# Products that nothing reads in two stretches of TensorE, and expert weights moved behind the exponent queries, in a two-layer gated cross-attention kernel

## The reference

```python
x = x + tanh(g_xattn[0]) * attention0(layernorm(x), ctx)            # softmax over 1500 keys
x = x + tanh(g_ffn[0])   * experts0(layernorm(x))                   # 8 experts, 128 -> 512 -> 128, gelu, top 2
x = x + tanh(g_xattn[1]) * attention1(layernorm(x), ctx, mask)
x = x + tanh(g_ffn[1])   * (experts1(layernorm(x)) + shared(layernorm(x)))   # 8 experts, 128 -> 64 -> 128
```

## Time and profile before

| | us |
|---|---|
| median of 3 runs | 1026.82 (1025.94 to 1027.41) |
| the profiled execution | 1026.83 |
| its span, first to last instruction | 1025.0 |
| PE busy | 905.8 (88%) |
| DVE busy | 731.6 (71%) |
| ACT busy | 588.3 (57%) |
| POOL busy | 518.1 (51%) |

### The profile page before, as it was taken

How to read it: one execution, slowest core, us unless ns; L and a number is a source line. 1 busy time by engine, 2 the same in 40 slices (tenths; PEclk the granted TensorE clock), 3 DMA queues, 4 the chain that set the end, 5 groups by cost and what they waited for, 6 DMA issues and landing times.

```text
span 1025.0 us, 32567 instructions
## 1 busy us (share of the span) xinstructions
PE 905.8 (88%) x13088; PEld 654.5 (64%) x13088; DVE 731.6 (71%) x1579; ACT 588.3 (57%) x1076; POOL 518.1 (51%) x662
## 2 busy tenths in 40 slices
PE   3887788898989899898999999999999999999975
PEld 1364576676766667677666777666666666666754
DVE  5665666777868678686775867788787878787723
ACT  1154547565575755757556575665657675757560
POOL 5542436643545445354744556666657666672211
PEclk9997899999999999999999999999999999999995
DMA  5324451222212222212665666677566666675300
GB/s 140 89 81 136 140 152 37 84 69 80 70 51 72 73 80 80 67 53 67 138 121 101 124 119 147 131 144 155 127 153 131 137 130 148 140 139 94 59 2 19
DMA packets 100291, 104.47 MB, mean 102 GB/s; under 512 B 28251, under 2 KB 93101, under 8 KB 100141
## 3 DMA queue, kind: packets, MB, share of 16 engines
q1 hardware_dynamic: 98722, 102.07, 42.6%
q10 hardware_dynamic: 1418, 0.32, 0.2%
HBM read 35.89 MB, written 0.46 MB: 35 GB/s over the span
## 4 chain that ended last, share of the span: by engine, by line
PE 57%; DVE 25%; ACT 9%; issue 7%; DMA 1%; SPq 0%; ACTq 0%; DVEq 0%
DVE mx L1056 13%; PE pO L1191 13%; PE pMX L1212 10%; PE pST L1170 8%; PE pKV L1257 6%; PE pKV L1248 6%; PE pFH L1379 5%; PE pFY L1311 3%; ACT P L773 3%; DVE rden L998 2%; ACT HR L782 2%; ACT L773 2%; DVE HR L954 2%; PE pFY L1315 2%; DVE ysc L1027 1%
## 5 line engine op out<-in xcount | busy, mean ns | idle before, releaser
L1056 DVE TENSOR_REDUCE mx<-pMX 112x1 f32<-112x500 f32 x768 | 487.5, 669 | 133.9 <-PE pMX L1212 131.1
L773 ACT ACTIVATE P<-pST 125x448 f32<-125x448 f32 x768 | 389.4, 542 | 286.7 <-PE pST L1170 281.5
L1212 PE MATMUL pMX<-kop,qmax 48*112 48x500 f16 (+1 forms) x768 | 285.9, 412 | 47.9 <-DVE mx L1056 38.1
L1170 PE MATMUL pST<-qexp,kop 50*128 50x112 f16 (+2 forms) x3072 | 267.7, 216 | 20.3 <-issue 10.1
L1170 PEld LDWEIGHTS pST<-qexp,kop 50*128 50x128 f16 (+2 forms) x3072 | 184.3, 101 | 86.0 <-issue 30.8
L1191 PE MATMUL pO<-P,V 125*17 125x112 f32 x6144 | 189.0, 264 | 0.0
L1212 PEld LDWEIGHTS pMX<-kop,qmax 48*112 48x112 f16 (+1 forms) x768 | 97.9, 130 | 123.1 <-DVE mx L1056 59.0
L630 POOL CAST khi<-kfull 128x500 f16<-128x500 f32 x96 | 57.9, 603 | 206.5 <-ACT kfull L800 205.1
L1191 PEld LDWEIGHTS pO<-P,V 125*17 125x17 f32 x6144 | 138.4, 98 | 35.0 <-issue 19.3
L632 POOL TENSOR_TENSOR klo<-kfull,khi 128x500 f16<-128x500 f32 x96 | 109.0, 1136 | 7.8
L721 POOL TENSOR_TENSOR Clo<-C,Chi 128x500 f16<-128x500 f32 x93 | 106.0, 1139 | 7.5
(11 more groups left out here) (152 smaller groups left out, 1112.8 us busy)
## 6 DMA issues: line engine op xcount, KB each, us to landing
C<-in_ctxT SPq DMA_DIRECT2D x31, 750.0 KB, 5.8
kop<-maskop SPq DMA_DIRECT2D x48, 437.5 KB
kop<-khi SPq DMA_DIRECT2D x192, 62.5 KB
kop<-khi SPq DMA_DIRECT2D x96, 125.0 KB
kop<-klo SPq DMA_DIRECT2D x96, 62.5 KB
kop<-klo SPq DMA_DIRECT2D x48, 125.0 KB
maskin<-in_mask SPq DMA_DIRECT2D x8, 656.2 KB, 5.9
qexp<-qmax SPq DMA_DIRECT2D x16, 182.0 KB
```

The source lines that it names most:

```text
L773: nc.scalar.activation(P[0:KP, slot, h * 4 * T:(h + 1) * 4 * T], pST[0:KP, h, 0:4 * T], ACT.Exp, scale=EXP_SCALE).then_inc(exp_done, 1)
L1056: nc.vector.tensor_reduce(mx[:, s % 2, c, p:p + 1], pMX[0:T, m % 2, 0:CW], AX.X, ALU.max).then_inc(max_done, 1)
L1170: mm = nc.tensor.matmul(pST[0:keys.stop - keys.start, h, i * T:(i + 1) * T], kop[rows, b, slot, keys], qexp[rows, b, slot, :, :].rearrange ...
L1212: nc.tensor.matmul(pMX[0:T, m % 2, 0:CW], qmax[rows, b, slot, :, :].rearrange("r j q -> r (j q)"), kop[rows, b, slot, c * CW:(c + 1) * CW] ...
```

## The change

Five groups of edits.

- **Fillers.** `keep_busy(bank, n)` issues n products of a 128 x 128 identity with 512 columns (fp16) into a PSUM bank that nothing reads at that time; no wait and no signal. In step 0 eight go ahead of round 0, two ahead of rounds 1, 3, 5, 7 and 11; in steps 33 and 34 `in_gap` names how many follow which small product.
- **Expert weights.** Loads of one expert each (256 KB) go right behind `qexp<-qmax`: `w1a` in steps 1 and 2, `w2a` in 3 and 4; `w1b` in step 5, `w2b` in 6. PE waits for them by pairs of experts. Biases and the first mask stay in `late_loads(1)`.
- **Start.** The first transfer brings `wk0` and `wq0`. The query weights and biases are no longer scaled; `head_of` holds 4.0 instead of 1.0, so that q is scaled as it is masked. The reordering of `wq0` is done by ACT after its first context piece. Key piece 0 of batch 0 is issued ahead of the context of batch 1.
- **Constants.** `late_constants` is split: `masks()` runs behind `other_weights()` in step -1, `output_biases()` (8 + 2 operations) in round 8 of step 1. Their loads move on ACT from round 11 of step 0 to round 8 of step -1.
- **Waits.** The counts follow from the above.

```diff
+def in_gap(s, use):
+    return {(NB + 1, "sum"): 5, (NB + 1, "y3"): 10, (NB + 1, "xT"): 2, (NB + 1, "h1"): 10,
+            (NB + 2, "gT"): 2, (NB + 2, "y1"): 3}.get((s, use), 0)
...
-            sp.dma_start(W[:, 0:D], wpack[:, 0:D]).then_inc(wk_in, 16)
+            sp.dma_start(W[:, 0:2 * D], wpack[:, 0:2 * D]).then_inc(wk_in, 16)
...
                 if s == 1:
...
-                    sp.dma_start(w1a[:, 0:E0 // 2, :], w1_0[0:E0 // 2].rearrange("e d f -> d e f")).then_inc(f_in, 16)
                     sp.dma_start(maskin[:, :], mask[0]).then_inc(mask_in, 16)
-                if s == 2:
-                    sp.dma_start(w1a[:, E0 // 2:, :], w1_0[E0 // 2:].rearrange("e d f -> d e f")).then_inc(f2_in, 16)
+            def expert_weights(s):
+                if s in (1, 2):
+                    for e in range(4 * (s - 1), 4 * s):
+                        sp.dma_start(w1a[:, e, :], w1_0[e]).then_inc(w1_in[e // 2], 16)
+                if s in (3, 4):
+                    for e in range(4 * (s - 3), 4 * (s - 2)):
+                        sp.dma_start(w2a[:, e, :, :], w2_0[e].rearrange("(c f) d -> f c d", c=F0C)
+                                     ).then_inc(w2_in[e // 2], 16)
+                if s == 5:
                     sp.dma_start(w1b[:, :, :], w1_1.rearrange("e d f -> d e f")).then_inc(f2_in, 16)
+                if s == 6:
                     sp.dma_start(w2b[:, :, :], w2_1.rearrange("(c e) f d -> (e f) c d", e=2)).then_inc(f2_in, 16)
-                if s == 3:
-                    for half in (slice(0, E0 // 2), slice(E0 // 2, E0)):
-                        sp.dma_start(w2a[:, half, :, :], w2_0[half].rearrange("e (c f) d -> f e c d", c=F0C)
-                                     ).then_inc(f3_in, 16)
...
                                      ).then_inc(qexp_in[s % 2], 16)
+                expert_weights(s)
+                if s == -1:
+                    key_chunk(st, 1, 0)
...
+                if c == 0:
+                    act.wait_ge(init_k, 2)
+                    nc.scalar.activation(w("wk0").rearrange("d (h r p) -> d h r p", r=PR, h=2),
+                                         w("wq0").rearrange("d (r h p) -> d h r p", r=PR, h=2), ACT.Copy).then_inc(init_q, 1)
...
-                if s == 0 and kt == 11:
+                if s == -1 and kt == 8:
...
-                nc.vector.memset(head_of[quarter, 0, k % 2:k % 2 + 1], 1.0).then_inc(init_h, 1)
+                nc.vector.memset(head_of[quarter, 0, k % 2:k % 2 + 1], QK_SCALE).then_inc(init_h, 1)
...
-                scaled("wq0", 2 * D).then_inc(init_v, 1)
-                dve.wait_ge(init_v, 3)
-                dve.wait_ge(init_k, 2)
-                nc.vector.tensor_copy(w("wk0").rearrange("d (h r p) -> d h r p", r=PR, h=2),
-                                      w("wq0").rearrange("d (r h p) -> d h r p", r=PR, h=2)).then_inc(init_b, 1)
...
-                    if s == 2 and kt == 2:
-                        late_constants()
+                    if s == 1 and kt == 8:
+                        output_biases()
...
+            def keep_busy(bank, n):
+                for _ in range(n):
+                    nc.tensor.matmul(bank[:, 0, :], ident16[:, :], Whi[:, :, :, :].rearrange("p l m n -> p (l m n)"),
+                                     start=True, stop=True)
...
+                    if s == 0:
+                        keep_busy(pST, 8 if kt == 0 else 0 if kt in (2, 4, 6, 8, 9, 10) else 2)
...
                         small(use)
+                        keep_busy(pMX, in_gap(s, use))
...
                             mm.then_inc(fh_ready, 1)
+                            keep_busy(pMX, in_gap(s, use))
```

More of the change, by code:

```diff
@@ L391, in build @@
         x0_in, c0_in = sem("x0_in"), [sem(f"c0_in{c}") for c in range(CH)]
-        w_in, x_in, f_in, f2_in, f3_in, wo_in = sem("w_in"), sem("x_in"), sem("f_in"), sem("f2_in"), sem("f3_in"), sem("wo_in")
+        w_in, x_in, f_in, f2_in, wo_in = sem("w_in"), sem("x_in"), sem("f_in"), sem("f2_in"), sem("wo_in")
+        w1_in, w2_in = [sem(f"w1_in{i}") for i in range(4)], [sem(f"w2_in{i}") for i in range(4)]
         c_in = sem("c_in")
@@ L395, in build @@
         init_chi = sem("init_chi")
-        init_k, init_b, init_clo = sem("init_k"), sem("init_b"), sem("init_clo")
+        init_k, init_q, init_b, init_clo = sem("init_k"), sem("init_q"), sem("init_b"), sem("init_clo")
         chi_done = sem("chi_done")
@@ L473, in _ @@
                 sp.dma_start(C[:, c * CW:(c + 1) * CW], ctxT[0, :, c * CW:(c + 1) * CW]).then_inc(c0_in[c], 16)
-            sp.dma_start(W[:, D:], wpack[:, D:]).then_inc(w_in, 16)
+            sp.dma_start(W[:, 2 * D:], wpack[:, 2 * D:]).then_inc(w_in, 16)
             sp.dma_start(X[:, D:].rearrange("t (g d) -> t g d", g=G - 1),
@@ L481, in late_loads @@
                 if s == 1:
+                    sp.wait_ge(init_w, 4)
                     sp.dma_start(b2x[0:NE, 0, :], b2_0).then_inc(f_in, 16)
@@ L564, in step @@
                 if has_k(s):
-                    key_chunk(st, 1, 0)
+                    if s >= 0:
+                        key_chunk(st, 1, 0)
                     if has_q(s) and s >= 0:
@@ L761, in early_loads @@
                         act.dma_start(bvE[rows, :, :], bvc.rearrange("l g i r -> g i l r")[g]).then_inc(wo_in, 16)
+                if s == 0 and kt == 11:
                     act.wait_ge(bc_in, 16)
@@ L851, in _ @@
                 quarter = slice(32 * k, 32 * (k + 1))
-                nc.vector.memset(head_of[quarter, 0, k % 2:k % 2 + 1], 1.0).then_inc(init_h, 1)
+                nc.vector.memset(head_of[quarter, 0, k % 2:k % 2 + 1], QK_SCALE).then_inc(init_h, 1)
             for j in range(2):
-                nc.vector.memset(head_of[64 * j:64 * (j + 1), 1, j:j + 1], 1.0).then_inc(init_h, 1)
+                nc.vector.memset(head_of[64 * j:64 * (j + 1), 1, j:j + 1], QK_SCALE).then_inc(init_h, 1)
             def scaled(name, width):
@@ L899, in other_weights, with masks @@
                 split_weights(0, 1, init_c, 0)
-                dve.wait_ge(init_v, 5)
+                dve.wait_ge(init_v, 4)
                 for m in range(2):
                     split_weights(1, m, init_c, 2 + 2 * m)
-            def late_constants():
+            def masks():
+                dve.wait_ge(init_p, 12)
                 nc.vector.memset(ones[:, :], 1.0).then_inc(init_l, 1)
@@ L911, in late_constants, with output_biases @@
                 dve.wait_ge(init_l, 5)
+                for j in range(2):
+                    nc.vector.tensor_scalar(headmask[:, :, j, :], ones[:, :].rearrange("p (r q) -> p r q", r=2),
+                                            rowmask[:, j:j + 1], rowmask[:, 2:3], ALU.mult, ALU.add).then_inc(init_l, 1)
+            def output_biases():
                 dve.wait_ge(wo_in, 16 * 8)
                 dve.wait_ge(init_a, 1)
+                dve.wait_ge(init_l, 7)
                 for j in range(2):
@@ L1122, in step @@
                         low_context(0)
-                        query_weights()
+                        key_bias()
                         low_context(1)
@@ L1128, in step @@
                         other_weights()
+                        masks()
                     if has_q(s) and s + 1 >= B and kt == 2:
@@ L1217, in step @@
                 if s == 0:
-                    pe.wait_ge(init_v, 5)
+                    pe.wait_ge(init_v, 4)
                     pe.wait_ge(init_c, 6)
@@ L1221, in step @@
                     pe.wait_ge(init_l, 17)
-                    pe.wait_ge(f_in, 16 * 5)
-                if s == 4:
-                    pe.wait_ge(f2_in, 16 * 3)
+                    pe.wait_ge(f_in, 16 * 4)
+                if s == 8:
+                    pe.wait_ge(f2_in, 16 * 2)
                 def free(sem_, uses, name):
@@ L1296, in small @@
                     else:
-                        if use == "y0" and s == 4:
-                            pe.wait_ge(f3_in, 32)
+                        if s == 4 or s == 5:
+                            pe.wait_ge(w2_in[int(use[1])], 32)
                         if use == "y0" or use == "y1" and layer_of(s - 3) == 0:
@@ L1334, in step @@
                         small("y1")
+                        keep_busy(pMX, in_gap(s, "y1"))
                         score_half(st, kt, 0)
@@ L1369, in step @@
                             if s == -1:
-                                pe.wait_ge(init_b, 3)
+                                pe.wait_ge(init_q, 1)
+                                pe.wait_ge(bias_in, 16 * 5)
                             nc.tensor.matmul(pFH[:, 0:T], wq, xnqT[:, :], start=True, stop=False)
@@ L1376, in step @@
                             l = layer_of(s - 2 if s % 2 else s - 3)
+                            if s == 3 or s == 4:
+                                pe.wait_ge(w1_in[e // 2], 32)
                             if l == 0:
```

9 lines of the change are left out of this document (3 added, 6 removed).

## The result

The changed kernel takes 1014.32 us, median of 4 runs (1012.67 to 1015.93), against 1026.38 us (1024.52 to 1027.41) for the kernel before: a ratio of 0.9884, 95% interval 0.9861 to 0.9908. It is faster, as forecast, but by 12 us instead of 33, and 1014.32 lies above the range, which ended at 1008. The profiled execution took 1013.41 us with a span of 1011.6 us, 13.4 us less than the span before.

A forecast was written before the change was run, and what follows sets the result against it. Early steps and the end were taken as bound by PE's waits, mainly for small ct transfers behind bulk loads, and the low clock behind them. Gains 2.7 + 3.5 + 5.0 + 7.5 + 5.4 + 4.4 + 4.5 = 33.0 gave 993.8 us, range 986 to 1008.

The forecast's parts named there:

- the place of the expert weights: Steps 3 and 4: no bulk load ahead of ct, so waits and low clock shrink; gains 5.4 and 4.4 us.
- The third rival: Weights in four small transfers hold up context and keys, about 2 us in each of four steps; 1001.8 us, chance 0.08.
- The start: Up to the first maximum product: less DVE work and waiting brings q earlier; gain 2.7 us, bounds 1.5 and 3.5.
- I take -3.5 us, a rise early in step 0: Step 0: fillers raise the clock early, making projections and maximum products faster; 3.5 us gained.
- the first rival: Step 0's fillers don't raise the clock; step 0 loses 3.4 us, step 1 0.8; 1006.5 us, chance 0.25.
- my best case: Step 0: full clock from the outset, -6.0 + 1.7 = -4.3 us.
- if the clock is up on entry: Step 1: full clock gives 6 us, less 1 us for moved output biases; gain 5.0 us.
- the term of the clock: Step 2: a shorter stall no longer takes the clock down, so low-clock work shrinks; 4 us of the 7.5 gained.
- wrong if a fall follows the mask in step 2: Step 2: sign against the forecast, which expected about 25 us and no low clock there.
- The fourth rival: Steps 2 to 4: ct late for another reason, stalls and low clock stay; 15.5 us less gain, 1009.3 us, chance 0.06.
- fillers at full clock, at 0.22 us each: The end: fillers hold the clock, saving 5.2 us for 0.7 us of cost; gain 4.5 us.
- The second rival: The end falls to the lower clock despite fillers: 7.0 us lost instead of 4.5 gained; 1005.3 us, chance 0.08.

The follow-up runs named there:

- the spread kernels: Changed kernel with context load first, step 0's fillers spread behind maximum products, with or without fillers in step 1: 1002.57 us with, 1005.61 us without.
- the kernel with all that helped: Changed kernel with context load first, spread fillers in steps 0 and 1, and denser fillers at the end: 996.75 us, ratio 0.9704 to the kernel before.
- the last two kernels: The kernel with all that helped, 996.75 us, and the same with the first mask's load moved to step 4, 998.98 us.

## Why the prediction was right in part, and wrong in its sum

**Right: the place of the expert weights.** Steps 3 and 4 gained 5.4 and 4.2 us where 5.4 and 4.4 were forecast. The working was that the bulk load ahead of `ct` makes the wait and the wait takes the clock down; the kernel with the old place shows both again. How much of it was the wait and how much the low clock behind it isn't shown: in steps 3 and 4 both went together. The cost of the 16 issues was put at nothing and was nothing: in steps 3 and 4 PE's waits for DMA are too short to be listed, and its longest wait of any kind is 0.7 us. The third rival (small transfers slow) is refuted by the kernel with single large ones, 1015.94 against 1014.32 us. Its premise, four landings one behind the other (12.4 us), was wrong: a group is in after some 5.7 us.

On that rival the Trainium skill, "DMA: Bandwidth & Descriptors", section "Bandwidth", had its rule of at least 1 MiB a transfer. No run here shows a loss from it: a 256 KB transfer takes 3.7 us, a 1024 KB one 5.8 us, and the kernel's time is the same.

**The start: the term was mis-sized, since one edit was left out of it.** The prediction took q, its issue and its landing to move together, and it gave no price to key piece 0 going ahead of the context load. In the timeline of SP in the kernel before, that load is issued well ahead of the queries, which go out from 15.55 us:

```profile
12.38 0.33 SPq L563 DMA_DIRECT2D C<-in_ctxT  x1
12.82 1.34 SPq L514 DMA_DIRECT2D kop<-khi  x2
```

The change moved it to 15.38 us, into the midst of the queries. The earlier issue is real (16.29 instead of 19.85 us at its end); the landing gave 2.7 of the 3.5 us back. With the context first the first maximum product is at 18.57 us, 3.5 us earlier than before, and at 18.13 us without fillers ahead of it: more than the forecast. What was missed is the very thing the prediction used for `ct`: a small urgent transfer behind bulk.

**Step 0: the step that failed is "I take -3.5 us, a rise early in step 0".** The rise came, earlier than I had hoped: the first maximum product took 0.42 us. What I didn't ask is what follows the rise. The eight fillers end at 19.0 us, then PE stands 2.29 us for the late queries, then come maximum products with waits for DVE between them; the clock is low again from 23 us on. With the context first the eight have no wait behind them, only the sparse maximum products, and the clock falls all the same, 3.4 us after its rise at 18.1 us. From there the first rival's price applied: a pair takes 1.0 us (26.33 to 27.32) instead of 0.43, with DVE waiting. It was bounded at +3.4 us; measured are +2.1 us (27.23 against 25.15 us without fillers). The size of the term was right for a clock that holds: 20.5 us in the spread kernels is -4.8 us, where my best case was -4.3.

**Step 1** failed with it, by the same sentence ("if the clock is up on entry"). It was up at 48.5 us, but fell at 50.3. The stretch ahead of that holds only maximum products and the waits for DVE's maxima: PE is busy for 3.46 of the 5.63 us from 44.57 to 50.20 us. With one or two fillers behind each product there PE is busy 5.39 of 5.66 us, and step 1 takes 23.17 us where the clock holds: -5.4 us, for a forecast of -5.0. It held in two of the three traces with these fillers. So the terms of steps 0 and 1 were right in size and wrong in their condition.

**Step 2: the term of the clock was mis-sized.** The constants went as forecast: PE's waits for DVE there fell from 3.6 to 1.6 us (forecast 1.8 less). The wait for `ct` fell from 4.30 to 3.15 us instead of to 2.5. Together that is 3.1 of the 3.4 us gained. The 4 us for the clock did not come: low for 10.2 us instead of 13.6. The prediction named this itself ("wrong if a fall follows the mask in step 2"), and gave it too little chance. In all kernels with the mask load in its place and the weights behind the queries the wait is 2.8 to 4.2 us, so a gain of 1.8 us there was too much to ask while the mask stood ahead of `ct`. The fourth rival was thus true for step 2 and false for steps 3 and 4; I had tied the three together.

**The end: the step that failed is "fillers at full clock, at 0.22 us each".** They were given to the waits that the profile showed as long, and those between the five fillers and `y` (0.57, 0.85, 0.45 us) were left open. The clock fell there at 985.5 us, before the ten after `y3`; these then cost 3.85 us, where I had counted 2.2, and kept `xT` back. The second rival priced a clock that stays low throughout (+7.0 us); in fact it rose behind the ten, and the whole came out even. With the short waits filled it takes 25.4 us from the end of `sum`, for which the prediction said 26.

**The sum.** Where the clock holds, the terms come out within 1.3 us of their forecast: in the kernel with all that helped they are -2.7 at the start, -4.8, -5.7, -4.8 (step 2, forecast -7.5), -4.9 and -4.4 in steps 0 to 4, and -5.2 at the end. That is 32.5 us of the forecast 33.0; what step 2 lacks (2.7 us) the others make up for. The span of that trace is only 28.9 us shorter than before, since the middle gives 3.7 us back in three short falls of the clock. The forecast gave the middle nothing, as its code is the same. The kernel takes 996.75 us, the forecast was 993.8; it has the context load, the fillers of steps 0 and 1 and those of the end in other places than the change, so it tests the sizes of the terms and doesn't make the forecast right. The fault was in the chances. I treated the rivals as one or another; the first, the second and the fourth each came true in part, at once, since all three come down to one doubt: whether the clock holds over waits that are only partly filled, or only shortened. Three terms (3.5, 5.0, 4.5 us) and the 4 us for the clock of step 2 hung on it.

## What to carry to other kernels

A small transfer that PE waits for costs what stands ahead of it or goes out with it, whatever queue it is on: put bulk loads behind the last urgent issue of a step, and when one is moved, look up who is next. Products that nothing reads paid here where they filled nearly all the waits of a stretch, one or two at a time behind each waiting product; one block ahead of a wait or of sparse work raised the clock and lost it again, and what followed then stood on the path at twice its price. Even the filled stretch held in two of three traces, so measure several executions before such a gain is counted. When several terms of a forecast depend on one condition, give that condition a chance of its own, and let the terms fall together.

## What the runs showed of the hardware that was not expected

- **The clock falls although PE keeps issuing.** In step 1 of the kernel after no wait is longer than 0.9 us in the 5.6 us before the fall at 50.3 us, and at the end none is longer than 0.85 us before 985.5 us. PE was busy for 3.46 of 5.63 us ahead of the one and 3.76 of 5.70 us ahead of the other. The prediction looked for stalls of 2 us and more. Few waits don't rule a fall out either: in the kernel with the mask in step 4 one came behind 5.05 busy us of 5.66, and in the middle of the kernel with all that helped one came behind 5.18 of 5.70. How busy PE must be isn't settled by these runs. The Trainium skill, "TensorE: Matmul & The Clock Gate", section "A second HAM failure mode: psum-queue depth-cycling", tells of a kernel whose short idle times between groups of products make the clock swing between its two levels. The traces here agree in so far as the clock fell with only short waits ahead of it.
- **A stretch held in one execution need not hold in the next.** Step 1 of the last two kernels has the same instructions; it took 22.85 us in one and 27.78 us in the other profiled execution. The times of two of the kernels with spread fillers range more widely (999.98 to 1009.34, 994.88 to 1002.87 us) than those of the kernel after (1012.67 to 1015.93). In the middle, too, the clock fell at other places, or not at all, with the same code: none to four times for 3.4 us, at 1.3 us each.
- **Transfers of another queue are held up too.** The queries are on ACT's queue, the context on SP's. The last of six transfers of 14 KB lands 5.0 us after its issue with the context beside it, near the time at which the context does (issued at 15.38, landing 5.6 us later), and 2.2 us after it in the kernel with the context first and no filler in step 0. How the two queues share the engines isn't shown.
